# Relational layers of a graph network: a ring of eight gathered batches, and row numbers copied one batch earlier at a tile's turn

## The reference, cut to what matters

```
def _rgcn_layer(x, W, root, bias, src, dst, seg):
    agg = jax.ops.segment_sum(x[src], seg, num_segments=N_REL * N_NODES)
    agg = agg.reshape(N_REL, N_NODES, -1)
    return jnp.einsum('rnd,rde->ne', agg, W) + x @ root + bias
seg = edge_type * N_NODES + dst
for l in range(N_LAYERS - 1):
    h = jax.nn.relu(_rgcn_layer(h, weights[l], roots[l], biases[l], src, dst, seg))
h = jax.nn.sigmoid(_rgcn_layer(h, weights[-1], roots[-1], biases[-1], src, dst, seg))
```

## Time and profile before

| | |
|---|---|
| median of three runs | 7211.5 us |
| profiled execution, its own time | 7188.47 us |
| its span (first to last instruction) | 7186.8 us |
| mean granted TensorE clock | 0.790 |
| layer 0, first gather to TensorE's last sum | 3524.5 to 4487.6 us |
| layer 1 | 4512.7 to 5476.3 us |
| layer 2 | 5503.0 to 6483.5 us |
| busy in the span: PE, DVE, POOL, ACT | 61%, 56%, 32%, 26% |
| gathers busy, layers 0, 1, 2 | 626.2, 626.1, 617.3 us |

### The profile page before, as it was taken

How to read it: one execution, slowest core, us unless ns; L and a number is a source line. 1 busy time by engine, 2 the same in 40 slices (tenths; PEclk the granted TensorE clock), 3 DMA queues, 4 the chain that set the end, 5 groups by cost and what they waited for, 6 DMA issues and landing times. The chain is left out here.

```text
span 7186.8 us, 83910 instructions
## 1 busy us (share of the span) xinstructions
PE 4353.8 (61%) x18940; PEld 2307.0 (32%) x18941; DVE 4000.0 (56%) x6280; ACT 1871.7 (26%) x2810; POOL 2289.1 (32%) x2170
## 2 busy tenths in 40 slices
PE   4888476133997165389756677566676444440387
PEld 2454375111443032174323333223332112220123
DVE  7987376698997599454322333222333122227898
ACT  1475111013885322244201111001111001110254
POOL 0000000500000065210266666566665666650000
PEclk8999687666998588699877889767887666665798
DMA  1471664434664277405555566555665444443444
GB/s 34 155 237 42 217 252 175 144 116 131 181 180 133 95 274 261 156 29 197 186 158 176 183 200 203 167 168 178 191 205 186 139 134 132 137 127 114 133 135 118
DMA packets 465578, 1145.77 MB, mean 159 GB/s; under 512 B 63211, under 2 KB 254210, under 8 KB 452828
## 3 DMA queue, kind: packets, MB, share of 16 engines
q1 hardware_dynamic: 293672, 550.53, 23.7%
q0 software_dynamic: 134816, 447.33, 21.0%
q10 hardware_dynamic: 36996, 146.80, 5.6%
HBM read 886.09 MB, written 261.55 MB: 160 GB/s over the span
## 5 line engine op out<-in xcount | busy, mean ns | idle before, releaser
L2682 POOL DMA_INDIRECT rel2s_rows<-rel_table,rel2s_at x640 | 617.3, 965 | 391.7 <-issue 222.2
L2682 POOL DMA_INDIRECT rel1s_rows<-rel_table,rel1s_at x640 | 626.1, 978 | 359.9 <-issue 277.4
L2682 POOL DMA_INDIRECT rel0s_rows<-rel_table,rel0s_at x640 | 626.2, 978 | 341.7 <-issue 282.1
L2884 PE MATMUL rel2s_acc<-rel2s_rows,rel2s_hot 128*128 x732 | 397.2, 553 | 491.4 <-issue 280.4
L2126 POOL TENSOR_TENSOR mamb_st<-mam_u,mamb_bc 128x1600 f32<-128x1600 f32 x64 | 230.9, 3608 | 1138.0 <-DMA mamb_bc<-dbc 1138.0
L1677 PE MATMUL gatx_acc<-gatx_w,gatx_feat 128*65 128x400 f32 x1600 | 541.5, 501 | 24.8 <-DVE gatx_w L1569 24.8
L2884 PE MATMUL rel1s_acc<-rel1s_rows,rel1s_hot 128*128 x732 | 319.6, 456 | 247.2 <-issue 173.5
L2884 PE MATMUL rel0s_acc<-rel0s_rows,rel0s_hot 128*128 x732 | 315.7, 451 | 240.9 <-issue 186.8
L1569 DVE SCALAR_TENSOR_TENSOR gatx_w<-gatx_w,gatx_adj 128x1600 f32<-128x1600 f32 x200 | 363.9, 1820 | 0.5 <-ACT gatx_w L1625 0.5
L1416 DVE CUSTOM_DVE_ANT_0 gatm_junk<-gatm_srow,gatm_gone 128x3200 bf16<-128x3200 f32 x100 | 343.5, 3489 | 33.5 <-DMA gatm_srow<-gat_scores 29.2
L1677 PE MATMUL latx_acc<-latx_w,latx_feat 128*65 128x400 f32 x800 | 291.7, 509 | 101.1 <-DVE latx_w L1569 101.1
(11 more groups left out here) (612 smaller groups left out, 9384.8 us busy)
## 6 DMA issues: line engine op xcount, KB each, us to landing
mamb_bc<-dbc SPq DMA_DIRECT2D x128, 800.0 KB, 5.8
agg_strip<-strips SPq DMA_DIRECT2D x100, 800.0 KB, 5.7
gatx_adj<-adj SPq DMA_DIRECT2D x200, 400.0 KB, 3.0
adj<-adj_counts SPq DMA_DIRECT2D x25, 1600.0 KB, 7.1
latx_adj<-adj SPq DMA_DIRECT2D x100, 400.0 KB, 3.1
rel_table<-rel0p_prod POOLq DMA_DIRECT2D x25, 1536.0 KB, 6.3
rel_table<-rel0s_prod ACTq DMA_DIRECT2D x25, 1536.0 KB
rel_table<-rel1s_prod ACTq DMA_DIRECT2D x25, 1536.0 KB
```

Of the source, the lines that this page charges most:

```text
L2682: pool.indirect_dma_start(rows[k][:, u, :], None, table, bass.IndirectOffsetOnAxis(ap=at[:, n:n + 1], axis=0)).then_inc(s_in[u], 16)
L2884: one = nc.tensor.matmul(acc[a][:, :], hots[k], most_two[k], start=fresh and k == 0, stop=False)
```

## The change

The ring of a layer has eight slots instead of four. With it grow the buffers for rows, row numbers, lanes and one-hot matrices, the loops of SyncE and GpSimd (unrolled eight times, so 20 passes instead of 40 for 160 batches), and the number of semaphores for gathers. GpSimd may gather batch q once TensorE has begun batch q - 7. At a tile's turn VectorE copies the row numbers of batch 2 in front of the eviction (and in front of `keep`); behind the eviction only the one-hot matrices of batch 1 are made. The row numbers of batch 3 are copied in the loop, as before.

```diff
-SLOTS = 4
+SLOTS = 8
@@ gather_sum, the vector engine's step
                 edges(t, first, 0)
+                numbers(step_start(nc, first + 2 * B))
                 if then and second:
                     keep(t - 2)
                 evict(t - 1, 1 - u, i)
-                edges(t, first, 1)
+                targets(step_start(nc, first + B), g.tile_base[:, bass.ds(t, 1)])
                 if then and second:
                     remainders(t - 2, u)
                     lowest(t - 2, u)
@@ program
-        g.pool_sems = [ctx.enter_context(nc.semaphore(f"pool_dma{n}")) for n in range(36)]
+        g.pool_sems = [ctx.enter_context(nc.semaphore(f"pool_dma{n}")) for n in range(48)]
```

## The result

The changed kernel took 7503.76 us (median of four runs, 7499.19 to 7520.93) against 7207.1 us for the kernel before on the same chip (7202.43 to 7221.27). The ratio is 1.0416, 95% interval 1.0399 to 1.0432: slower by 4.2%. The forecast was slower, by 1.4%, with 7450 us as the upper end.

What follows compares the result with a forecast made beforehand. GpSimd's gather queue and its pauses bound the kernel. Tiles 7 to 24 (+67, +65, +1) and 1 to 6 (-18, -1, -10) give +104 us on 7188.5, 7292; that execution ran 23 below the median, so 7315 us, range 7120 to 7450.

Steps and rivals of the forecast that it cites:

- What bounds the kernel: GpSimd's one queue: each layer is 800 us of gathers plus about 150 us of pauses; the change acts on the pauses.
- nothing: Rival, chance 0.09: TensorE, catching up after each pause, sets the pace over a tile, so pauses only move; 7211 us.
- The reading of the late counts: TensorE's counts arrive at once in a young unbroken gather stream, later are held until some 3.4 us after it breaks.
- the forecast's 3.37: At a held turn, the us from the break in GpSimd's gathers to the start of the eviction.
- The price of a turn: GpSimd's cost where the sum is held: 10.9 us in layers 0 and 1, 8.25 in layer 2, against 4.9 before.
- How many turns are held: Of 18 turns before tiles 7 to 24, seven (after tiles of six or more) and about 6.5 of eleven: 13.5.
- The formula 5.0 (n - 3) + 3.5 us: When TensorE ends a tile of n batches, counted from the stream's restart at batch 3: 8.5 us for n = 4.
- the limit of 17.2 us for an escape: Latest eviction start in the stream for a turn to cost nothing: 25.0 - 0.84 - 6.97, batches lasting 25 us.
- Tiles 1 to 6: Each layer's first stretch: four of five turns held, two stops inside tiles of 4.3 us; changes -18, -1, -10 us.
- Worse than forecast: Rival, chance 0.07: the hold after a break grows with the stream and every turn is held; 7490 us.
- counts at 3 us a turn: Low bound: counts get through on their own, about 3 us a turn; -27 us a layer, 7080 to 7100 us.
- the first rival: Counts come through, chance 0.11: eight slots end the hold, every pause goes, 447 us, 6765 + 23; half left, about 7000.

## Why the prediction was wrong, point by point

*What bounds the kernel.* Right in the main. The layers are 321 us longer of the span's 332.5, and GpSimd's pauses are nearly all of it. But in layers 0 and 1 TensorE had a hand in how long the pauses are, which the forecast had under "nothing" alone.

*The reading of the late counts.* Right in its condition, as far as the runs go: with breaks every 10 us the counts are in time, and they are late whatever the bytes. In the traces with late counts no sum that fell into a running stream more than 15.4 us after its last restart was in time. But how long a stream must be is not a sharp number: in the changed kernel a sum at 15.4 us was in time in layer 2, and one at 8.4 us in layer 0 was 14.4 us late. In tiles 7 to 24 held counts came 2.8 to 3.8 us after the break in layers 0 and 1, near the forecast's 3.37, and 3.8 to 5.3 us after it in layer 2. Four more in layer 2 came 0.9 to 7.0 us late while the stream still ran.

*The price of a turn.* Right in layers 0 and 1 for turns at which the count was held: 10.9 us were forecast, 10.4 measured, and the run with the copy behind the eviction shows that the additions in between are part of the price. The mean over all eighteen turns is 205 / 18 = 11.4, for a reason that follows. In layer 2, 8.25 us were forecast and the mean is 150 / 18 = 8.3, but that is luck: seven held turns at 8.7 to 10.5 us, and eleven of another kind at 5.8 to 8.2.

*How many turns are held.* This is the step that failed: "of the other eleven about 6.5 are". GpSimd paused in front of batch 3 at all eighteen turns of each layer, and by more than one way.

In layers 0 and 1 all eleven sums behind tiles of four and five batches were held, for 7.4 to 14.8 us. The formula 5.0 (n - 3) + 3.5 us had its 3.5 from rows of layer 2 in which TensorE kept up. After a pause of 10 us, and with layer 0's table work, it does not. It gets the one-hot matrices of batch 1 only behind the eviction, and then has batches 1 and 2 and the table work to do (busy 17.5 of the 19.3 us from the eviction to the sum in the first turn shown above). So tiles of four ended their sums 11.9 to 14.5 us into the stream instead of 8.5, and tiles of five at 13.9 to 21.4 instead of 13.5, and none of their counts was prompt. Also, the limit of 17.2 us for an escape is that of a tile of five; for a tile of four the same sum gives 20.0 - 0.84 - 6.97 = 12.2 us.

At the seven turns behind tiles of six batches and more, which the forecast had as held, no count of a sum was held in layers 0 and 1: each eviction came 0.2 us after TensorE. At six of the seven TensorE itself was late, with evictions 4.3 to 8.4 us after the break and prices of 11.3 to 15.4 us, as in the second turn shown above. The seventh is a stop inside the tile and a shorter one at the turn, together some 11 us. The price was there, but not for the reason given.

In layer 2 the seven were held, for 13.9 to 16.0 us. Of the other eleven the forecast's timing was near (10.2 us for tiles of four), seven came in time and four 0.9 to 7.0 us late, so at least as many escaped as the 4.5 of the forecast. But what stands behind the eviction was looked at only for its length (4.34 us), not for its own wait on a late count. The run with the sigmoid first shows it. Together this is 58 + 58 + 39 = 155 us over the forecast in tiles 7 to 24.

*Tiles 1 to 6.* 52, 52 and 42 us were forecast, 87, 65 and 75 measured, 81 us more. In layer 0 the five turns cost 10.7, 10.5, 10.0, 8.4 and 11.0 us (none came free; the last two are each a stop before the eviction and one behind it, and the fourth's count was in time), and there were four more stops inside tiles where two were forecast, of 4.7 to 6.0 us where 4.3 were. The forecast had a stream run for about ten batches before such a stop; in layer 0 it stopped seven batches after a restart each time, one more than before. 13 us more in this layer, before and after alike, are the wait for the first gather, which the forecast's 52 had left out.

*TensorE's faltering*, 146 and 125 us of idle time in layers 0 and 1, was not in the forecast, and stands behind the longest turns (14.5 and 15.1 us, in front of tiles 7 and 9). At the six late turns of each layer, evictions later than 3.4 us after the break add up to some 16 us a layer (an estimate from the timelines). What it is worth in all I cannot separate: no run takes it away and leaves the long streams.

*The rivals.* "Worse than forecast", every turn held at 7490 us, with a chance of 0.07, is nearest to what happened, and its price was near (7504 us measured). Its mechanism, a hold that grows with the stream, is there in layer 2 alone; that the number fits is in part luck. Its chance was far too low, for the escapes rested on a timing and on one wait, and neither was worked out for the state in which the change leaves TensorE and ScalarE. Two sums of the better cases were off as well: 7211 less 447 is 6765, without another 23; and with counts at 3 us a turn layer 2 would lose 56 us, not 27, so some 7050 us.

*Outside all of it:* that the kernel before can run in 6765 us. Nothing in the one trace said so. It is also what the first rival's sum gives for no pause at all.

## What to carry to other kernels

Where an engine waits for a count that comes only after another has paused, a deeper ring does not remove the pause, it moves it to the next thing that stands behind the wait; so list, for the new stop, everything between the wait and what releases it, with the waits of each of these and not only their lengths. A ready time read from a stretch in which an engine keeps up doesn't hold after a longer pause: work out anew what it has to catch up. And when a pause has no cause in the program, look at the same kernel in several executions before building on it.

## What the runs showed of the hardware

With gathers issued from GpSimd every 1.25 us, TensorE's semaphore counts can reach the other engines 8 to 16 us late (changed kernel), and TensorE itself can stand idle between two matmuls for 1.7 to 2.9 us. It depends on the unbroken stream (no sum's count over 1.4 us late with breaks every 10 us, against up to 16.4 without), not on the bytes (92 or 182 GB/s) nor on the number of counts (half, once, twice). It is there in some executions and not in others of the same kernel (7195 or 6767 us), on one chip at one time and not at another; what decides it stays open.

Executions with late counts also leave fewer semaphore events in the trace (44,750 against 71,280 for the kernel before), which may be why so many releasers there carry the name of an unrelated transfer. Every execution timed here has a span and a clock on record, so it was being recorded as it ran; whether the recording has a part in the lateness is a rival that no run here tests.

A third finding is smaller: the counted loop in VectorE's program, given an empty range, ran once (in layers 0 and 1 165 copies of row numbers instead of 160, with five tiles of four batches).
